# One-hots of an edge stage divided between VectorE and ScalarE, by pairs of units

## The reference, cut to what matters

```python
h = relu(layernorm(x))
xn = layernorm(h) * ln_w + ln_b
w_phys = (silu(rbf @ w1 + b1) @ w2 + b2) * cutoff[:, None]     # per edge
msg_phys = xn[col] * w_phys
Q, K, V = xn @ wq + bq, xn @ wk + bk, xn @ wv + bv             # per node, 8 heads
scores = sum(Q[row] * K[col], -1) / sqrt(32) * cutoff[:, None]
attn = softmax(scores, axis=1)                                 # over the 8 heads of an edge
combined = msg_phys + gate * (attn[..., None] * V[col])
aggr = segment_sum(combined, row, n)
out = x + h + aggr @ wo + bo
```

## Time and profile before

| | us |
|---|---|
| median of 3 runs | 5721.61 |
| lowest and highest | 5720.52, 5729.41 |
| the profiled execution | 5727.87 |
| its span | 5726.1 |

### The profile page before, as it was taken

One profiled execution on the slowest core, in us unless ns is written; L12 is line 12 of the kernel. 1 busy time (PEld: TensorE's weight loads), 2 busy tenths in 40 slices (PEclk: granted clock), 3 DMA queues, 4 the chain that ended last, 5 costly groups with the idle time before them and its releaser, 6 DMA issues. The chain is left out here.

```text
span 5726.1 us, 115218 instructions
## 1 busy us (share of the span) xinstructions
PE 5242.1 (92%) x24352; PEld 3838.2 (67%) x24353; DVE 4458.7 (78%) x7861; ACT 3117.6 (54%) x9962; POOL 4114.1 (72%) x3476
## 2 busy tenths in 40 slices
PE   3889999999999999996899999999999999999999
PEld 3556666666666666664666666666666666666667
DVE  8889976666655554226899999999999999999995
ACT  4546565666666666563455555555555555555553
POOL 1567777777777777675777777777777777777770
PEclk9989999999999999997999999999999999999999
DMA  6234354444444444438999999999999999999955
GB/s 196 90 109 150 121 169 165 156 134 157 165 155 142 150 166 159 142 125 299 312 307 303 305 308 304 303 305 303 308 305 306 307 307 304 304 306 306 308 185 180
DMA packets 584396, 1306.11 MB, mean 228 GB/s; under 512 B 81246, under 2 KB 384134, under 8 KB 582961
## 3 DMA queue, kind: packets, MB, share of 16 engines
q0 software_dynamic: 221536, 881.08, 44.2%
q1 hardware_dynamic: 311796, 345.48, 20.4%
q10 hardware_dynamic: 50850, 77.03, 3.7%
HBM read 1024.15 MB, written 324.38 MB: 236 GB/s over the span
## 5 line engine op out<-in xcount | busy, mean ns | idle before, releaser
L1029 POOL DMA_INDIRECT ukvx<-kvx_table,urec x1760 | 2302.3, 1308 | 705.0 <-issue 640.5
L339 POOL DMA_INDIRECT records<-rows,slot_i x1660 | 1743.9, 1051 | 682.8 <-issue 468.5
L694 PE MATMUL w_ps<-w2s,hid 128*128 128x256 f32 x6656 | 1553.9, 387 | 51.3 <-DVE rows L608 51.1
L694 PEld LDWEIGHTS w_ps<-w2s,hid 128*128 128x128 f32 x6656 | 1249.9, 193 | 375.3 <-issue 156.5
L608 DVE TENSOR_TENSOR rows<-w_ps,b2b 128x512 f32<-128x512 f32 x832 | 571.3, 687 | 744.1 <-PE w_ps L694 743.9
L1131 PE MATMUL ag_ps<-ukvx,uonehot 128*128 128x256 f32 x3520 | 987.3, 403 | 153.5 <-DVE ukvx L1203 78.2
L1111 PE MATMUL uq_ps<-aggr,uonehotT 128*128 x3520 | 974.9, 400 | 0.3 <-issue 0.3
L808 ACT ACTIVATE hid<-hid_ps,b1t 128x512 f32<-128x512 f32 x832 | 525.4, 682 | 820.9 <-PE hid_ps L683 806.2
L1134 PE MATMUL ag_ps<-ukvx,uonehot 128*128 128x256 f32 x3520 | 906.5, 380 | 1.0 <-DVE ukvx L1236 1.0
L1060 ACT ACTIVATE uexp<-uscores,umax 128x8 f32<-128x8 f32 x1760 | 507.5, 289 | 649.2 <-DVE umax L1220 649.1
L1131 PEld LDWEIGHTS ag_ps<-ukvx,uonehot 128*128 128x128 f32 x3520 | 600.1, 190 | 372.2 <-issue 273.9
(11 more groups left out here) (174 smaller groups left out, 4629.6 us busy)
## 6 DMA issues: line engine op xcount, KB each, us to landing
urec<-records SPq DMA_DIRECT2D x880, 260.0 KB, 6.3
rbf_in<-in_edge_attr SPq DMA_DIRECT2D x207, 256.0 KB, 3.0
kvx_table<-kvx ACTq DMA_DIRECT2D x10, 3456.0 KB, 14.5
ukvx<-kvx_table,urec POOLq DMA_INDIRECT x1760, 5.9
records<-rows,slot_i POOLq DMA_INDIRECT x1661, 2.1
records<-kvx SPq DMA_DIRECT2D x1, 13000.0 KB
aggr<-query_table SPq DMA_DIRECT2D x7, 1792.0 KB, 20.1
fbase<-x_plus_h SPq DMA_DIRECT2D x14, 896.0 KB, 7.2
```

The lines of the kernel that those rows point to most:

```text
L339: pool.indirect_dma_start(recs, bass.IndirectOffsetOnAxis(ap=slot_i[:, q, t:t + 1], axis=0), rows[:, q, t, :], None).then_inc(scattered[q] ...
L694: m = pe.matmul(w_ps[j % 2][:, h, :], hid[:, k % 2, c, h, j * P:(j + 1) * P], w2s[:, c, :], start=(h == 0 and c == 0), stop=(c == 1), skip ...
L1029: pool.indirect_dma_start(kvx[:, k, j, :], None, table, bass.IndirectOffsetOnAxis(ap=rec[:, k, j, R_DST:R_DST + 1].bitcast(I32), axis=0), ...
```

## The change

For the units in slots 0, 1, 4 and 5 VectorE's comparison makes the one-hots as before. For those in slots 2, 3, 6 and 7 ScalarE makes them: `spread` writes |iota - place| with one Abs activation per half, five units ahead, and `pick` writes relu(1 - that) with one Relu activation over both halves, four units ahead. The semaphore `onehot_ready` is replaced by `paired` (VectorE's, counted by four per pair) and `picked` (ScalarE's, by two per unit), and `spread`; whoever waited for the first now waits for one of the others, by slot.

```diff
--- before.py
+++ after.py
@@ -929,6 +929,7 @@
         kvx = sb("ukvx", [P, DEPTH, 2, TAB])
         iota_bf = sb("uiota_bf", [P, P], BF16)
         ohb = sb("uonehot_bf", [P, DEPTH, 2, P], BF16)
+        one = sb("uone", [P, 1])
         ident_bf = sb("uident_bf", [P, P], BF16)
         oh = sb("uonehot", [P, DEPTH, 2, P])
         ohT = sb("uonehotT", [P, 4, 2, P])
@@ -941,7 +942,7 @@
         ag_ps = ps("ag_ps", [P, SUMS, H])
 
         s = {n: sem("u_" + n) for n in (
-            "zeroed", "narrow", "blank", "rec_waited", "onehot_ready", "widened", "turned", "ohT_ready", "qe_done",
+            "zeroed", "narrow", "blank", "rec_waited", "paired", "spread", "picked", "widened", "turned", "ohT_ready", "qe_done",
             "qk_done", "phys_done", "scored", "weighted", "max_done", "exp_ready", "recip_done", "shared",
             "av_done", "ag_waited", "ag_done", "kept", "q_waited", "named")}
         rec_in = [sem(f"u_rec_in{k}") for k in range(DEPTH)]
@@ -949,7 +950,7 @@
         q_in = sem("u_q_in")
         kvx_in = [sem(f"u_kvx_in{k}") for k in range(DEPTH)]
         TURNS = UNITS // DEPTH
-        GATHER_AHEAD, SELECT_AHEAD, TURN_AHEAD, OUT_AHEAD, ASK_AHEAD = 5, 4, 3, 2, 2
+        GATHER_AHEAD, SPREAD_AHEAD, SELECT_AHEAD, TURN_AHEAD, OUT_AHEAD, ASK_AHEAD = 5, 5, 4, 3, 2, 2
         rec_v = recs.rearrange("(u j p) f -> u p j f", p=P, j=2)
         q_v = queries.rearrange("(b p) f -> p b f", p=P)
 
@@ -982,6 +983,12 @@
             for k in range(DEPTH):
                 body((TURNS - 1) * DEPTH + k, k, TURNS - 1, False, True)
 
+        def chosen(eng, u, k):
+            if k % 4 < 2:
+                eng.wait_ge(s["paired"], u + 1)
+            else:
+                eng.wait_ge(s["picked"], u)
+
         def ahead(fn, n, u, k, i, first, last):
             if not (last and k + n >= DEPTH):
                 fn(u + n, (k + n) % DEPTH, i + (k + n) // DEPTH, first and k + n < DEPTH)
@@ -1006,7 +1013,7 @@
                 if not first:
                     sp.wait_ge(s["phys_done"], u - (DEPTH - 1))
                     sp.wait_ge(s["weighted"], u - (DEPTH - 1))
-                    sp.wait_ge(s["onehot_ready"], u - (DEPTH - 1))
+                    sp.wait_ge(s["paired" if k % 4 < 2 else "picked"], u - (DEPTH - 1))
                 sp.dma_start(rec[:, k], rec_v[u] if isinstance(u, int) else rec_v[bass.ds(u, 1)].rearrange("a p j f -> p (a j) f")).then_inc(rec_in[k], 16)
                 if first and k == 2:
                     ask_first(0, q_first[0])
@@ -1045,8 +1052,25 @@
                     act.wait_ge(s["qe_done"], u - 3)
                 act.activation(ohT[:, k % 4], turn_ps[:, 0:2, :], ACT.Copy).then_inc(s["ohT_ready"], 1)
 
+            def spread(u, k, i, first):
+                if k % 4 < 2:
+                    return
+                act.wait_ge(rec_in[k], i * 16 + 16)
+                if not first:
+                    act.wait_ge(s["widened"], u - (DEPTH - 1))
+                    act.wait_ge(s["turned"], u - (DEPTH - 1))
+                for j in range(2):
+                    m = act.activation(ohb[:, k, j, :], iota_bf[:], ACT.Abs, scale=-1.0, bias=rec[:, k, j, R_LOC:R_LOC + 1])
+                m.then_inc(s["spread"], 2)
+
+            def pick(u, k, i, first):
+                if k % 4 < 2:
+                    return
+                act.wait_ge(s["spread"], u)
+                act.activation(ohb[:, k], ohb[:, k], ACT.Relu, scale=-1.0, bias=one[:, 0:1]).then_inc(s["picked"], 2)
+
             def widen(u, k, i, first):
-                act.wait_ge(s["onehot_ready"], u + 1)
+                chosen(act, u, k)
                 if not first:
                     act.wait_ge(s["ag_done"], u - (DEPTH - 1))
                 act.activation(oh[:, k], ohb[:, k], ACT.Copy).then_inc(s["widened"], 1)
@@ -1071,6 +1095,11 @@
 
             act.activation(half_asked[:], half_bucket[:, HPAD:HPAD + HALVES], ACT.Copy).then_inc(s["named"], 1)
             bucket_of = [None] * 4
+            act.wait_ge(s["narrow"], 3)
+            for k in range(SPREAD_AHEAD):
+                spread(k, k, 0, True)
+                if k:
+                    pick(k - 1, k - 1, 0, True)
             for k in range(OUT_AHEAD):
                 evacuate(k, k, 0, True)
                 widen(k, k, 0, True)
@@ -1082,6 +1111,8 @@
                 ahead(widen, OUT_AHEAD, u, k, i, first, last)
                 if k % 2:
                     exponent(u, k, i, first)
+                ahead(spread, SPREAD_AHEAD, u, k, i, first, last)
+                ahead(pick, SPREAD_AHEAD - 1, u, k, i, first, last)
                 if not (first and k < LAG):
                     keep(u - LAG, bucket_of[k % 2 * 2])
             turns(act, unit)
@@ -1096,7 +1127,7 @@
         @block.tensor
         def _(pe):
             def turn(u, k, i, first):
-                pe.wait_ge(s["onehot_ready"], u + 1)
+                chosen(pe, u, k)
                 if not (first and k == 0):
                     pe.wait_ge(s["ohT_ready"], u)
                 for j in range(2):
@@ -1189,7 +1220,7 @@
                     dve.wait_ge(s["widened"], u - (DEPTH - 2))
                     dve.wait_ge(s["turned"], u - (DEPTH - 2))
                 dve.tensor_tensor(pair(ohb, k), iota_bf[:].unsqueeze(1).to_broadcast([P, 4, P]),
-                                  pair(rec, k)[:, :, R_LOC:R_LOC + 1].to_broadcast([P, 4, P]), ALU.is_equal).then_inc(s["onehot_ready"], 2)
+                                  pair(rec, k)[:, :, R_LOC:R_LOC + 1].to_broadcast([P, 4, P]), ALU.is_equal).then_inc(s["paired"], 4)
 
             def query_key(u, k, i, first):
                 q = k % 2
@@ -1235,13 +1266,13 @@
                 values = pair(kvx, k - 1)[:, :, H:2 * H].rearrange("p r (h d) -> p r h d", h=NH)
                 dve.tensor_tensor(values, values, ex[:, q].unsqueeze(3).to_broadcast([P, 4, NH, HD]), ALU.mult).then_inc(s["av_done"], 2)
 
+            dve.memset(one[:], 1.0).then_inc(s["narrow"], 1)
             dve.tensor_copy(ident_bf[:], ident[:]).then_inc(s["narrow"], 1)
             dve.tensor_copy(iota_bf[:], iota1[:]).then_inc(s["narrow"], 1)
             for k in range(GATHER_AHEAD):
                 dve.memset(kvx[:, k], 0.0).then_inc(s["blank"], 1)
-            dve.wait_ge(s["narrow"], 2)
-            for k in range(0, SELECT_AHEAD, 2):
-                select(k, k, 0, True)
+            dve.wait_ge(s["narrow"], 3)
+            select(0, 0, 0, True)
             dve.memset(zeros_bf[:], 0.0).then_inc(s["zeroed"], 1)
             dve.memset(ag_ps[:], 0.0).then_inc(s["zeroed"], 1)
             for k in range(GATHER_AHEAD, DEPTH):
@@ -1258,7 +1289,8 @@
                     score(u, k, i, first)
                     weigh(u, k, i, first)
                     maximum(u, k, i, first)
-                    ahead(select, SELECT_AHEAD - 1, u, k, i, first, last)
+                    if (k + SELECT_AHEAD - 1) % 4 == 0:
+                        ahead(select, SELECT_AHEAD - 1, u, k, i, first, last)
             turns(dve, unit)
             U = UNITS
             before = (U - 1, DEPTH - 1, TURNS - 1, False)
```

## The result

Measured beside each other, the kernel before took 5725.5 us (5720.5 to 5731.9, 4 runs) and the changed one 5624.65 us (5615.6 to 5627.05, 4 runs). The ratio is 0.982, with a 95% interval of 0.980 to 0.984: faster by 101 us where 108 were forecast. The profiled execution of the changed kernel took 5615.6 us (span 5613.9), that of before 5727.9 (span 5726.1). The edge stage itself, from the start of TensorE's first transposition to the start of its last sum, shrank from 3011.9 to 2905.9 us.

The account below looks back on a forecast made before the run. VectorE was taken to bound the edge stage. Gains of 68 + 34 + 11 = 113 us, less 5 near the start, leave 108: 5721.6 - 108 = 5614 us, own range 5590 to 5635, wider range 5565 to 5672.

Parts of the forecast that it names:

- The bound: Edge stage: VectorE sets the pace, waiting for no other engine; its turn falls from 27.0 to 26.0 us.
- Slot 3: VectorE, end of slot 3: without the comparison the product follows the maximum after 0.22 instead of 0.84 us, gaining 0.62.
- Slot 7: VectorE, before the loop's jump: the jump loses its cover, so removing the comparison gains only 0.31 us, bounds 0 to 0.62.
- Rival (a): VectorE at the loop's jump: the jump stays hidden as the sequencer runs ahead; gain 142 us, time 5580, chance 0.12.
- The average extra: VectorE, 220 removed comparisons: mean idle before a comparison exceeds that at the place read, adding 0.05 us each, 11 us.
- Start and prologue: Near the stage's start about five transfer-bound turns give back nothing, 5 us; the prologue counts as nothing, within 5 us.
- ScalarE's cost: ScalarE's new activations: 0.39 us per 128 columns, 0.50 for the wide one, 1.28 us per unit.
- ScalarE's slack: ScalarE's waits of 3.27 us per pair hide the new steps; both shrink but stay, the evacuation about in time.
- TensorE: Edge stage: TensorE isn't the next bound, 23.9 us a turn against VectorE's 26.0; it waits for comparisons only at slots 1 and 5.
- Transfers: Edge stage: transfers aren't the next bound; 304 GB/s would become 316, and short windows reached 372.
- Rival (b): GpSimd takes over, its gathers lengthened beside VectorE's multiplications; gain 55 us, time 5667, chance 0.15.
- Rival (d): ScalarE: the first Abs waits for its record, copies and evacuation queue behind it; slower, 5788 us, chance 0.07.

Follow-up runs that it names:

- idle comparisons at one slot each: Changed kernel plus a VectorE comparison that nobody waits for or reads, at slot 7 alone: 5648.4 us; at slot 3 alone: 5673.1 us.
- row "none": The changed kernel once more, nothing added, as base beside the runs with an extra comparison: 5625.5 us, ratio 0.9826 against the kernel before.
- the work alone: Against the kernel before, ScalarE also does its new steps into a tile nobody reads, VectorE keeping all comparisons: 5726.5 us, ratio 0.9998.

## Why the prediction was right

The forecast of 5614 us lies 11 us under the median of 5624.65, inside its own narrower range; as a gain, 108 us against 101. (That the profiled execution lies only 1.6 us from it is chance: it was the fastest of four.) The mechanism held; that the sum came so near is in part luck, since one term of 11 us had no ground and the two main ones were 7 us too small. Point by point:

- **The bound.** Right. VectorE's saving came out one to one: 1.00 us of rows, 1.00 us of turn; and time put back on VectorE came back in the time (+23, +48, +74).
- **Slot 3.** 0.62 forecast, 0.66 measured: the product follows a maximum after 0.18 us, not 0.22. A register step and one wait in front of it were taken to cost what two waits cost in front of a comparison; they cost 0.04 us less.
- **Slot 7.** 0.31 forecast, 0.34 measured, for the reason given: the jump begins when the maximum is issued, and its steps show. Rival (a), a jump that stays hidden, would have given 0.66 at this place as well; it fell by the row with 0.30 us of "issue" and by the idle comparisons at one slot each.
- **The average extra.** 0.05 us at each of 220 places, 11 us, was wrong. The mean idle before a comparison was above that of the places I had looked at because the comparisons at slots 1 and 5, which stayed, have a register step more (0.31 and 0.33 against 0.23). A mean over four places was credited to two that weren't like it. The term is zero; the two terms of the slots being 4 and 3 us larger than forecast made up for most of it: 110 x 0.66 + 109 x 0.34 = 110 us against 113.
- **Start and prologue.** 5 us off and zero were forecast. The edge stage's length fell by 106 us, against 110 from the turns. The first turns of the loop, in which record loads and gathers are late, are together 7.8 us longer than as many median ones before and 13.3 with the change (15.1 in the trace of the row "none"), so they keep back 5.5 us, as forecast. What is left lies within what executions differ by.
- **ScalarE's cost.** 0.39 and 0.50 forecast, 0.389 and 0.496 measured. In the loop it is hidden altogether (ratio 0.9998 with the work alone).
- **ScalarE's slack.** The wait before the evacuation went from 1.83 to 126.5 / 353 = 0.36 us per pair, "about in time" as said. That both waits would shrink was wrong: the one before the exponent grew, from 491.2 / 340 = 1.44 to 597.7 / 353 = 1.69 us per pair. The exponent had more room than I gave it.
- **TensorE.** It waits for comparisons only twice in a turn, slots 1 and 5, and isn't the bound even at a turn of 24.6 us, where it is busy 973 of 1,000 us: VectorE has no wait for its products there. Transfers: 316 GB/s forecast, 316 measured.
- **Rival (b), GpSimd.** It fell by the opposite of what it supposed. GpSimd's gathers got shorter, and at times it now waits for TensorE to free a buffer:

```profile
4008.02 1.00 POOL L1036 DMA_INDIRECT ukvx<-kvx_table,urec  x1 [1.83 <-PE ag_ps L1165]
4009.33 1.01 POOL L1036 DMA_INDIRECT ukvx<-kvx_table,urec  x1 [0.30 <-issue]
4010.89 1.47 POOL L1036 DMA_INDIRECT ukvx<-kvx_table,urec  x1 [0.55 <-issue]
```

- **Rival (d), an Abs that waits for its record.** In the steady 2,300 us line 1063 has no idle time before it, so its price wasn't asked there. Before 3000 us, where records are late for everyone, it waited for them 7 times, 28.2 us in all; what that cost isn't told apart from the 5.5 us above.

## What to carry to other kernels

When the waits say that one engine waits for nobody, work taken off it pays by what the *next* instruction gains, read at each place apart, and moving it pays even where the other engine needs almost four times as long for it, as long as that one's waits hold it. Look at what the removed instruction was covering: a loop's jump was worth half of the saving at one of two places. And don't credit the mean of a group to some of its members before seeing that they are alike.

## What was unexpected in the hardware

- **Gathers got faster without being touched.** In the same 2,300 us the mean gather went from 1315 to 1095 ns, and GpSimd's busy time in the whole run from 4114 to 3743 us. A gather takes 1.01 us clear of VectorE's two multiplications of 1,024 columns and 1.4 to 2.0 beside them. In the changed kernel fewer of them begin there: of the 1,362 gathers of the steady stretch before, 665 began inside such a multiplication and took 1.59 us on average, the others 1.05; of 1,414 with the change, 454 did and took 1.28, the others 1.01. That they begin elsewhere because buffers are freed at other moments (the 1.83 us above) is argued; no run set the phase on purpose.
- **Waits in front of an instruction.** Two of them cost a comparison 0.13 us, 0.23 against 0.10 us after the maximum; a register step in front cost 0.08 to 0.10 more.
- **The jump.** 0.30 us bare on VectorE, nothing under a comparison of 512 columns, behind which the next instruction starts 0.6 us later.
- **A body twice as long.** 388 instruction packets for 119, and on ScalarE 3.9 us without an instruction in each passage, behind the jump.
